# Splitting a folded 256x256 projection into two rank-8 factors, and rewriting the hand-made orders of all five engines

## The reference, cut to what matters

```
x_dbl = xc @ x_proj_w                      # 256 -> 40 features
dt, Bm, Cm = jnp.split(x_dbl, [DT_RANK, DT_RANK + D_STATE], axis=-1)   # 8, 16, 16
dt = jax.nn.softplus(dt @ dt_proj_w + dt_proj_b)                       # 8 -> 256
...
dA = jnp.exp(dt_t[..., None] * A)
h = dA * h + dt_t[..., None] * B_t[:, None, :] * x_t[..., None]
```

## Time and profile before

| | us |
|---|---|
| median of 3 runs | 1353.74 (1352.81 to 1356.07) |
| the profiled execution, its time | 1361.48 |
| its span | 1359.7 |
| PE busy | 1145.5 (84%) |
| DVE busy | 988.0 (73%) |
| ACT busy | 747.5 (55%) |
| mean granted clock of PE | 0.939 |

### The profile page before, as it was taken

The page is one execution under the profiler, slowest core; times in us unless marked ns, Lnnn a source line. Parts: engine busy times, 40 slices in busy tenths (PEclk is TensorE's granted clock), DMA queues, the critical chain, the costliest instruction groups (busy, mean ns, idle before and its releaser), DMA issues.

```text
span 1359.7 us, 27149 instructions
## 1 busy us (share of the span) xinstructions
PE 1145.5 (84%) x10384; PEld 781.7 (57%) x10384; DVE 988.0 (73%) x1563; ACT 747.5 (55%) x1325; POOL 272.9 (20%) x262
## 2 busy tenths in 40 slices
PE   6587768878988799988997899889998899888677
PEld 4354444545765567655764566656665567656455
DVE  3143245797678977897777877899677978788796
ACT  2233444664657565866567565665557565654442
POOL 1000002152022322043022232124112411023200
PEclk9787797889999899999999899899999899979799
DMA  7620011000310112110320031100310121002010
GB/s 210 145 60 1 2 39 23 2 17 29 95 40 17 28 68 57 35 33 17 75 68 2 17 81 42 52 32 28 92 37 2 48 76 52 33 32 71 4 62 20
DMA packets 117517, 62.66 MB, mean 46 GB/s; under 512 B 79440, under 2 KB 99440, under 8 KB 117392
## 3 DMA queue, kind: packets, MB, share of 16 engines
q1 hardware_dynamic: 113488, 54.68, 14.8%
q10 hardware_dynamic: 3904, 6.26, 1.4%
HBM read 53.56 MB, written 6.83 MB: 44 GB/s over the span
## 4 chain that ended last, share of the span: by engine, by line
PE 57%; DVE 20%; issue 10%; ACT 9%; DMA 3%; POOL 1%; SPq 0%; ACTq 0%; DVEq 0%; POOLq 0%
PE strips L787 9%; PE strips L772 8%; PE attn_out L800 7%; PE ps L968 6%; DVE rowmax_B L1322 6%; PE ps L980 6%; ACT probs L1087 4%; DVE hb L1457 3%; DVE rowmax_A L1322 2%; PE ps L823 2%; DVE hb L1449 2%; DVE hb L1464 2%; PE ps L911 2%; PE ps L730 2%; PE ps L890 1%
## 5 line engine op out<-in xcount | busy, mean ns | idle before, releaser
L1087 ACT ACTIVATE probs<-strips 128x2048 f32<-128x2048 f32 x128 | 240.2, 1877 | 108.8 <-PE strips L787 108.3
L1322 DVE TENSOR_REDUCE rowmax_B<-strips 128x8 f32<-128x2048 f32 x96 | 219.5, 2286 | 90.7 <-PE strips L772 89.8
L1457 DVE TENSOR_TENSOR_SCAN hb<-da,hb 128x1024 f32<-128x1024 f32 x64 | 156.9, 2452 | 2.5 <-ACT da L1171 0.8
L980 PE MATMUL ps<-ze,w_e 128*128 128x256 f32 x512 | 140.1, 403 | 8.8 <-DVE hb L1464 2.5
L787 PE MATMUL strips<-qs_b,ks_b 32*128 32x256 f32 x1536 | 120.4, 430 | 23.1 <-ACT probs L1087 13.0
L772 PE MATMUL strips<-ks_b,qs_b 32*128 32x256 f32 x1536 | 117.0, 420 | 26.0 <-ACT probs L1087 12.7
L968 PE MATMUL ps<-w_e,work 128*128 128x128 f32 x1024 | 133.0, 286 | 3.5 <-DVE hb L1449 1.1
L968 PEld LDWEIGHTS ps<-w_e,work 128*128 128x128 f32 x1024 | 126.6, 200 | 13.7 <-issue 10.5
L1171 ACT ACTIVATE da<-dt,a_neg 128x255 f32<-128x255 f32 x256 | 108.0, 498 | 24.3 <-DVE hb L1457 23.9
L1654 POOL TENSOR_TENSOR cv_t<-hb 128x512 f32<-128x512 f32 x49 | 62.4, 1273 | 275.5 <-DVE hb L1464 275.5
L1218 ACT ACTIVATE eh_t<-ps 128x512 f32<-128x512 f32 x128 | 74.8, 594 | 74.7 <-PE ps L980 74.0
(11 more groups left out here) (239 smaller groups left out, 1825.7 us busy)
## 6 DMA issues: line engine op xcount, KB each, us to landing
w_e<-in_w_e SPq DMA_DIRECT2D x128, 256.0 KB, 2.9
qs_a<-a_scr SPq DMA_DIRECT2D x8, 512.0 KB, 3.8
ks_a<-a_scr SPq DMA_DIRECT2D x8, 512.0 KB, 4.9
pos<-t_scr ACTq DMA_DIRECT2D x16, 192.0 KB
a_scr<-qkv_a SPq DMA_DIRECT2D x16, 128.0 KB, 4.3
qs_b<-maxrow SPq DMA_DIRECT2D x96, 4.0 KB
x_in<-in_x SPq DMA_DIRECT2D x8, 128.0 KB, 2.4
a_scr<-ks_a SPq DMA_DIRECT2D x2, 512.0 KB, 6.5
```

What stands on the lines that cost most here:

```text
L980: mm = pe.matmul(o[:, j * L:(j + 1) * L], w_e1[:, n % RING, f * P:(f + 1) * P], ze[:, b % 2, :], start=True, stop=True)
L1087: act.activation(probs[:, group % 2, :, :, :].rearrange("p h a b -> p (h a b)"), strips[:, :], ACT.Exp).then_inc(s_exp, 1)
L1322: dve.tensor_reduce(out=rowmax[kind][:, b % sides_n, k % 2, :, :], in_=strips[:, :].rearrange("p (h q t) -> p h q t", h=4, q=2), axis=AX, ...
L1457: dve.tensor_tensor_scan(flat_h, flat_a, flat_h, 0.0, ALU.mult, ALU.add).then_inc(scan_done.of(b), 1)
```

## The change

Three things change. First, `dt` is made in two steps. The 8 features of rank are 8 more output rows of the `bc` matmuls (96 to 104). A new ACT stage `dt_rank` copies these 8 rows from PSUM to `dt_low` in SBUF. A PE stage `dt` of its own multiplies them with the 8x256 factor: 2 matmuls with a contraction of 8, where there were 4 with 128. DVE's `bc` waits for the copy before its second operation. Second, `dt_fold` is gone, with one of the two small loads (`N_LOADS` 16 to 15). Third, all five order strings and `BANKS` are written anew.

```
-LAYER1 += [("inproj",), ("conv",), ("xc",), ("bcdt",), ("bc",), ("dtx",)]
+LAYER1 += [("inproj",), ("conv",), ("xc",), ("bcdt",), ("dt_rank",), ("bc",), ("dt",), ("dtx",)]
...
-        w_bc = sb("w_bc", [P, CH, 96])
-        w_dt = sb("w_dt", [P, CH, CH * P])
+        w_bc = sb("w_bc", [P, CH, 96 + RANK])
+        w_dt = sb("w_dt", [96 + RANK, CH * P])[96:96 + RANK, :]
+        dt_low = sb("dt_low", [96 + RANK, L])[96:96 + RANK, :]
...
-                "bcdt": lambda: [("bc", bc_steps, 1), ("dt", dt_done, 0)],
+                "bcdt": lambda: [("bc", bc_steps, 1)],
+                "dt": lambda: [("dt", dt_done, 0)],
...
-            def dt_fold(b, k):
-                o = take(b, ("dt_fold", k))
-                pe.matmul(o[:, 0:CH * P], raw_dtt[:, k * P:(k + 1) * P], raw_dtw, start=True, stop=True).then_inc(s_ps, 1)
...
                 for k in range(CH):
-                    mm = pe.matmul(o[0:96, 0:L], w_bc[:, k, :], xc[:, k, :], start=(k == 0), stop=(k == CH - 1))
-                mm.then_inc(s_ps, 1)
+                    mm = pe.matmul(o[0:96 + RANK, 0:L], w_bc[:, k, :], xc[:, k, :], start=(k == 0), stop=(k == CH - 1))
+                mm.then_inc(s_ps, 1)
+
+            def dt_full(b):
+                pe.wait_ge(*rank_done.at(b))
                 o = take(b, "dt")
                 for m in range(CH):
-                    for k in range(CH):
-                        mm = pe.matmul(o[:, m * L:(m + 1) * L], w_dt[:, k, m * P:(m + 1) * P], xc[:, k, :], start=(k == 0), stop=(k == CH - 1))
+                    mm = pe.matmul(o[:, m * L:(m + 1) * L], w_dt[:, m * P:(m + 1) * P], dt_low[:, :], start=True, stop=True)
                 mm.then_inc(s_ps, 1)
...
-            def bcdt(b):
+            def dt_rank(b):
+                ready(act, b, "bc")
+                if b:
+                    ready(act, b - 1, "dt")
+                act.activation(dt_low[:, :], bank(b, "bc")[96:96 + RANK, 0:L], ACT.Copy).then_inc(rank_done.of(b), 1)
+
+            def dt_soft(b):
                 ready(act, b, "dt")
...
                 dve.wait_ge(*bc_steps.at(b, 0))
+                dve.wait_ge(*rank_done.at(b))
                 dve.tensor_tensor(bc_rem[:, :], o, bc3[:, :], ALU.subtract).then_inc(bc_steps.of(b), 1)
```

More of the change, by code:

```diff
@@ L83 @@
     FOLD += [("fold", _c), ("bias", _c)] + ([] if _c else [("table",)])
[L84 removed]
+FOLD += [("bias_end",), ("w12",), ("bias_ff",)] + [("consts",)]
 LANES = {"fold": FOLD, "cell": CELL, "side": SIDE, "raw": RAW, "one": LAYER1, "two": EXPERTS}
@@ L88 @@
     "sync": "load rows t_rows a_write a_stack v_read o_write o_read weights store",
-    "tensor": "fold bias bias_end w12 bias_ff dt_fold table prep_t q k v max rows score values post_b post_a ctx node aproj values_a gather wo_y ab_t ff_y "
-              "z_t inproj bcdt state spread_c sum x2 h_t ffn ffn_out router expert expert_y",
+    "tensor": "fold bias bias_end w12 bias_ff table prep_t q k v max rows score values post_b post_a ctx node aproj values_a gather wo_y ab_t ff_y "
+              "z_t inproj bcdt dt state spread_c sum x2 h_t ffn ffn_out router expert expert_y",
     "scalar": "table pos prep_t q k v rows exp out ctx node aproj values_a gather ab_t "
-              "z_t inproj xc bcdt state h_t ffn ffn_t router expert",
-    "vector": "fold bias bias_end w12 bias_ff dt_fold consts prep_stats prep_apply top post_b post_a end_y end_apply end_x wo_y wo_apply ff_y ff_apply "
+              "z_t inproj xc dt_rank dt state h_t ffn ffn_t router expert",
+    "vector": "fold bias bias_end w12 bias_ff consts prep_stats prep_apply top post_b post_a end_y end_apply end_x wo_y wo_apply ff_y ff_apply "
               "n0_stats n0_apply n1_stats n1_apply n2_stats n2_apply inproj conv xc bc state scan mix y x2 ffn ffn_t ffn_out router rank expert expert_y total",
@@ L983, in _ @@
             run_stages("tensor",
-                       {"fold": fold, "bias": bias, "bias_end": bias_end_, "w12": w12_, "bias_ff": bias_ff_, "dt_fold": dt_fold, "table": table, "prep_t": prep_t, "aproj": aproj, "q": queries, "k": keys, "v": values_in,
+                       {"fold": fold, "bias": bias, "bias_end": bias_end_, "w12": w12_, "bias_ff": bias_ff_, "table": table, "prep_t": prep_t, "aproj": aproj, "q": queries, "k": keys, "v": values_in,
                         "values_a": values_a, "max": maximum, "rows": max_rows, "score": score, "values": values,
```

102 lines of the change are left out of this document (48 added, 54 removed).

## The result

The kernel after the change takes 1368.35 us (median of 6 runs) against 1354.9 us of the kernel before on the same chip. The ratio is 1.0088, with a 95% interval of 1.0047 to 1.0129: slower by 0.9%. The prediction was 1344.0 us, with a range of 1335 to 1355. The profiled execution took 1371.5 us, its span is 1369.7.

A forecast was written before the change was run, and what follows sets the result against it. PE, busy 84%, was taken as nearest to a bound, though not everywhere. Start -9.0, PE -2.1, DVE +0.7, ACT +0.3, tail +0.4 sum to -9.7: from 1353.74 to 1344.0 us, 8-in-10 range 1335 to 1355.

The forecast's parts named there:

- factors and copy: At dt in eight batches: PE -2.1, DVE +0.7 and ACT +0.3 us, weighted by chain shares.
- the start: Seven stages moved ahead of `values_a@0` fill PE's 11.46 us wait for `va_hd`: -9.0 us, bounds 5 and 11.5.
- the tail: At b = 7: `expert.0` ahead of `inproj` +1.7, earlier `dt` -0.9, `total@6` behind `state.0@7` -0.4: +0.4 us.
- Rival 3: Other moved stages, three or four misplaced on the chain, give back 5 us, half the gain: 1349 us; chance 0.15.
- My sign that the prediction is wrong: The start's 9 us there at 80 us and gone by 250, or PE's waits at `dt` above 10 us.
- the walk: PE followed stage by stage through the start by row lengths: `score.B.3@0` at 79.7 us, 9.5 us earlier.
- Rival 1: The start gives nothing: the `va_hd` read lands up to 5.2 us later; 1353.0 us, chance 0.14.
- PE's work at dt: Four of eight matmul records per batch go at `dt`: 7.9 us of PE work removed.
- PE's net: At `dt`, work removed less 4.75 us of new waits for the copy: -3.1 us, times 0.67 is -2.1.
- The copy: ACT's `dt_rank` before `dt`: eight copies of 0.38 us, table loads staying 16; ACT's share +0.3 us.
- Rival 2: The copy holds up three queues, up to 3.3 us per batch, 26 on PE: 1363 us; chance 0.11.
- weights of 0.67 for PE and 0.20 for DVE: Mid-run, a microsecond of PE work removed is worth about 0.67 us, one added on DVE 0.20.

The follow-up runs named there:

- 2: Kernel before with only the two-step dt and its copy added, old order lists kept: 1361.08 us, ratio 1.0031.
- 3: Changed kernel with the new lists only for stages that start before 108 us, lists of before behind: 1345.45 us, ratio 0.9916.
- 4: Changed kernel with the new lists only for stages that start before 485 us, lists of before behind: 1348.94 us, ratio 0.9950.
- experiment 8: Kernel before, folded matrix kept and no copy, with the new lists for the first 108 us only: 1343.16 us, ratio 0.9883.
- 1: Kernel before, folded matrix kept and no copy, with the changed kernel's orders on all five engines: 1371.38 us, ratio 1.0114.
- Experiment 10: Kernel with factors and the new lists to 108 us only, its copy done four times in a chain per batch: 1364.74 us, ratio 1.0071.
- 7: Changed kernel with the lists of before put back for stages from 485 to 1145 us: 1348.51 us, ratio 0.9921.
- 11: Kernel before, folded matrix and no copy, with the new lists to 108 us and behind 1140 us: 1341.75 us, ratio 0.9894.
- 9: Changed kernel with one small block near 503 us put back towards the old order on TensorE, ScalarE and SyncE: 1365.31 us, ratio 1.0067.
- 5: Changed kernel with the new lists only up to 620 us, lists of before behind: 1362.69 us, ratio 1.0038.

## Why the prediction was wrong

**The parts, by experiments that differ in one thing each** (in brackets the 95% range of the difference):

```
                                            predicted    measured
factors and copy (2 against before)            -1.1        +5.7   (2 to 8)
new start, to 108 us (3 against 2)             -9.0       -15.6   (-20 to -12)
new lists 108 to 485 us (4 against 3)             0        +3.5   (0 to 8)
new lists from 485 us on (changed against 4)   +0.4       +19.4   (11 to 24)
sum                                            -9.7       +13.0
```

**The step that failed** is the last sentence on the start: "What is behind keeps nearly its order, so the whole rest of the run moves with it." The rest does keep nearly its order: only 19 of PE's stages move by more than five places. But the term for these moves, put at nothing but for +0.4 in the tail, measured 3.5 + 19.4 = 22.9 us, and 19.4 of it, behind 485 us, is far beyond the noise. In the two steps that were followed (503 and 560 us) the runs show in its place waits of PE that the old lists don't have, and in some executions a fall of its clock behind them. Rival 3 named the kind of loss ("Half is given back by other moved stages") and gave it 5 us and a chance of 0.15, by a price of 1 to 2 us for each of three or four misplaced stages. The runs show the sum to be four to five times as large; they do not show what one misplaced stage costs. My sign that the prediction is wrong (the gain "there at 80 us and gone by 250") looked in the right way at the wrong place: it was gone by 620.

**The start** was right in its mechanism, and the walk met the trace at its end: `score.B.3@0` at 79.09 where 79.7 was worked out. The wait in front of `values_a@0` was 5.92 us, and not 3 or less: PE was there at 59.5 us, where the walk had it near 63, and the walk itself, with the read landing at 67.17, would have left 4.2. The read landed by 65.4 us. The term was too small: 15.6 us against 9.0 (13.2, 8 to 21, with the folded matrix, experiment 8 against the 1356.34 us of its before), beyond the bound of 11.5. Where the surplus over the 10 us at `score.B.3@0` comes from was not looked for. Rival 1 did not happen; the read of `va_hd` did not land 5 us later.

**PE's work at dt.** 32 records with a median of 374 ns, where 379 was forecast; a contraction of 8 rows makes a record 5 ns shorter and no more. By the groups of lines `dt` was busy for 16.6 us and is now for 10.2, 6.4 less where I had 7.9, and `bc` rose from 8.5 to 9.6. PE's waits before `dt` sum to 5.5 us (3.4 of them for the copy) where I had 4.75. The longest is 1.4 us, at b = 0, and it is for DVE to read a bank; the longest for the copy is 1.3 us, at b = 2, where I had 1.75. So PE's net is about nothing, and not -3.1.

**The copy** was in no trace of before, and its length (0.376 us), its count and the 16 table loads came out as worked out. Rival 2's bound was not reached: PE's waits there are under 2.6 us a batch by far. Yet three pairs measure the factors at +5.7 (experiment 2 against before), +2.3 (3 against 8) and -3.0 us (the changed kernel against 1, where `bcdt` also stands elsewhere): about nothing to slightly bad. Only the first is clear of noise, and it goes against the -1.1 of the sum. Experiment 10 shows that time at this place is dear: added copies of 9.0 us cost 19.3. The weights of 0.67 for PE and 0.20 for DVE, taken from the shares of the chain, were too low there; one thing that they leave out is that the granted clock was lower with the longer waits. The wait at b = 2 that the prediction singled out is such a place in the changed kernel: 1.26 us, with the clock at 0.50 behind it. No run shows what they should be for a single copy.

**The tail** (+0.4) is not told apart by any run: experiments 7 and 11 against 4 and 8 give -0.4 and -1.4 us, within the noise.

**What stays open.** The two stretches behind 485 us are shown to lose by their new lists. No single move is shown to be a cause: the one block that was put back recovered nothing clear. Which moves cost the time, and whether it is their sequence or the banks that go with it, was not tried one by one. How the 11.6 us of the first stretch fall into cause and effect is shown only in part: the 4.8 us at the lower clock come in the same stretch as the 6.8 us of waits, the two steps show the clock falling right behind a wait, and experiment 10 shows that added waits bring such time with them.

## What to carry to other kernels

When a change brings a new order of stages, split it by time before you judge it: the old and the new lists can be joined at a point, and a few such joins told a gain of 13 to 16 us at the start from a loss of 19 us behind the middle. Do not cost moves at nothing because they are small or few: 28 moved stages of PE in one stretch, with those of the other engines there, cost 14 us. Do not take a wait that only the slower kernel shows for the cause either, before it is put right and timed: here the wait went and the time stayed. Compare such a step also in other kernels that share the same lists, since it came out at 2.1 and at 3.8 us under the same lists, by whether PE's clock fell. And once the pieces are known, ship only the good one: the new order of the first 108 us alone, with the folded matrix, is 1.2% faster than the kernel before.

## What the runs showed of the hardware

Longer waits of PE came with a lower clock. In experiment 10 PE waited 9.7 us more at `dt` and its 10348 records took 11.1 us longer, at a mean granted clock of 0.930 against 0.940; over all executions the clocks are 0.924 to 0.939 against 0.940 to 0.950. At single places the clock was at or near its lower level (0.50 and 0.55) right behind waits of 1.26 and 1.93 us, and at 1.00 behind waits of 0.89, 1.36 and 1.42 us at the same stages of other kernels; so the length of the last wait alone does not decide it. The Trainium skill (TensorE: Matmul & The Clock Gate, HAM oscillation — how this bites in real kernels) tells of a kernel in which waits for transfers between bursts of matmuls bring the clock down. The trace agrees with that direction, with shorter waits than in the page's case (15.2 us in eight of them).

The time to issue a transfer on SP's queue differs with what was issued just before. The small one of the row maxima took 0.53 us where no weight loads stood right ahead of it and its read (experiments 4 and 9), and 1.68, 0.99 and 0.96 us where two did (the changed kernel, experiments 5 and 1). Why it varies between these three is not shown.

Two executions of one kernel, the one before, lie 5 us apart at the same stages from 400 us on, and PE's busy time in them is 1145.5 and 1138.9 us at mean clocks of 0.939 and 0.938.
